# Third block of a four-block transformer: the norm's rows turned in the score-transposes' banks, projections in other slots, and another wait ahead of the MLP

## What is computed

```
ln_out = layernorm(x, ln1_s, ln1_b)
q, k, v = split(ln_out @ w_qkv + b_qkv)
x = x + merge(attention(q, k, v, ltor_mask)) @ w_ao + b_ao
ln_out = layernorm(x, ln2_s, ln2_b)
q = ln_out @ w_q + b_q
k, v = split(encoder @ w_kv + b_kv)
x = x + merge(attention(q, k, v, cross_mask)) @ w_co + b_co
ln_out = layernorm(x, ln3_s, ln3_b)
x = x + gelu(ln_out @ w1 + b1) @ w2 + b2
```

## Time and profile before

| | us |
|---|---|
| median of 3 runs | 1572.81 |
| profiled execution, its own time | 1579.1 |
| its span | 1577.3 |
| TensorE busy (matmuls) | 1481.9 |
| VectorE busy | 931.0 |
| ScalarE busy | 906.0 |
| POOL busy | 142.0 |

### The profile page before, as it was taken

How to read it: one execution, slowest core, us unless ns; L and a number is a source line. 1 busy time by engine, 2 the same in 40 slices (tenths; PEclk the granted TensorE clock), 3 DMA queues, 4 the chain that set the end, 5 groups by cost and what they waited for, 6 DMA issues and landing times.

```text
span 1577.3 us, 28655 instructions
## 1 busy us (share of the span) xinstructions
PE 1481.9 (94%) x9824; PEld 1140.7 (72%) x9824; DVE 931.0 (59%) x3314; ACT 906.0 (57%) x2807; POOL 142.0 (9%) x163
## 2 busy tenths in 40 slices
PE   7999999999999999999999999998888777999996
PEld 5766687788787877778788877786566556866664
DVE  4777723455554555445555445416999994168887
ACT  5888834434444444444444434435998895289996
POOL 2010010000000000000000000111122221022200
PEclk9999999999999999999999999999999999999999
DMA  7000103010010101001010000001000100000000
GB/s 288 1 2 2 59 5 120 1 48 15 1 62 1 62 1 47 15 1 61 1 47 16 1 1 1 1 1 54 1 2 8 41 9 7 1 1 8 22 2 15
DMA packets 10879, 40.66 MB, mean 26 GB/s; under 512 B 2416, under 2 KB 2672, under 8 KB 8688
## 3 DMA queue, kind: packets, MB, share of 16 engines
q1 hardware_dynamic: 10736, 38.82, 6.9%
HBM read 37.77 MB, written 1.05 MB: 25 GB/s over the span
## 4 chain that ended last, share of the span: by engine, by line
PE 68%; DVE 9%; ACT 9%; issue 3%; DVEq 0%; POOL 0%; POOLq 0%; ACTq 0%
PE bank L777 7%; PE bank L758 7%; PE bank L791 7%; PE bank L750 7%; PE bank L737 7%; PE bank L740 7%; ACT probs L948 6%; PE bank L706 5%; PE bank L717 5%; PE bank L766 4%; DVE probs L1201 3%; PE bank L562 3%; DVE probs L1183 3%; PE bank L549 2%; PE bank L584 2%
## 5 line engine op out<-in xcount | busy, mean ns | idle before, releaser
L948 ACT ACTIVATE probs<-probs,negmax 128x256 f32<-128x256 f32 (+1 forms) x640 | 347.3, 554 | 54.2 <-DVE negmax L1201 53.7
L1022 ACT ACTIVATE pT<-bank 128x512 f32<-128x512 f32 x128 | 76.4, 597 | 388.0 <-PE bank L766 388.0
L562 PEld LDWEIGHTS bank<-ident,probs 128*128 128x128 f32 x1536 | 170.4, 142 | 106.4 <-issue 52.1
L562 PE MATMUL bank<-ident,probs 128*128 128x128 f32 x1536 | 228.2, 282 | 19.4 <-ACT pT L956 14.9
L1334 DVE TENSOR_REDUCE stats<-bank 128x1 f32<-128x257 f32 x256 | 108.4, 425 | 212.4 <-PE bank L758 211.4
L1201 DVE CUSTOM_DVE_ANT_0 probs<-bank,mask_a 128x256 f32<-128x256 f32 (+1 forms) x384 | 174.2, 508 | 32.8 <-PE bank L549 28.1
L956 ACT ACTIVATE pT<-bank 128x512 f32<-128x512 f32 x288 | 169.8, 591 | 26.2 <-PE bank L562 25.3
L777 PE MATMUL bank<-pT,probs 128*128 128x256 f32 x512 | 132.7, 381 | 2.7 <-ACT pT L1022 2.7
L758 PE MATMUL bank<-kT,pT 128*128 128x257 f32 x512 | 132.7, 382 | 0.6 <-ACT pT L1005 0.6
L549 PE MATMUL bank<-kT,q_res 32*128 32x256 f32 (+1 forms) x1280 | 113.5, 460 | 19.7 <-DVE probs L1183 11.3
L948 ACT ACTIVATION_READ_ACCUMULATOR probs<-probs,negmax 128x1 f32 x640 | 129.3, 202 | 0.0
(11 more groups left out here) (110 smaller groups left out, 2485.4 us busy)
## 6 DMA issues: line engine op xcount, KB each, us to landing
w_m<-in_w SPq DMA_DIRECT2D x6, 1024.0 KB, 7.0
g_qkv<-in_g SPq DMA_DIRECT2D x4, 1536.0 KB, 7.6
q_res<-in_g SPq DMA_DIRECT2D x4, 1536.0 KB, 6.6
w_qkv<-in_w SPq DMA_DIRECT2D x3, 768.0 KB, 4.5
g_bv<-in_gbv SPq DMA_DIRECT2D x8, 256.0 KB, 7.2
g_o<-in_go SPq DMA_DIRECT2D x4, 512.0 KB, 3.4
q_res<-in_go SPq DMA_DIRECT2D x4, 512.0 KB, 3.5
rows<-in_rows SPq DMA_DIRECT2D x1, 1664.0 KB, 14.4
```

Of the source, the lines that this page charges most:

```text
L562: last = nc.tensor.transpose(out[:, n * P:(n + 1) * P], probs[:, u % PROBS, q * T + t * P:q * T + (t + 1) * P], ident[:, :])
L948: last = nc.scalar.activation(s, s, ACT.Exp, bias=negmax[:, u % PROBS, k:k + 1], scale=-1.0, accum_out=sums[:, tile % 2, q, j * c.res + r: ...
```

## The change

Within a part, q, k, y, v go to slots 1, 4, 8, 11. The norm's rows are turned at slot 2 (before: 1), for all parts but the last, in the bank into which that slot's unit is transposed afterwards (`turned_bank`, here always bank 5): TensorE waits for the copy of the unit two before, turns the rows, and the unit's transposes wait for ScalarE's take. ScalarE takes them before the exponential of slot 15 instead of behind that of slot 0. The last part's rows still use bank 7. The rows are written at the same VectorE slot (14), the bias added at the same POOL slot (15). In the MLP behind, slot 12 moves from f = 8 to f = 4, and TensorE waits at f = 0 for the masked products (`a_masked`) instead of the maxima.

```diff
     def y_slot(self, p):
-        return self.tile_slot(2 * p + 1) + (5 if self.kinds == "mult" else 4)
+        return self.tile_slot(2 * p + 1) + (2 if self.kinds == "mult" else 4)
     def norm_slot(self, p):
-        return self.y_slot(p) + 6
+        return self.y_slot(p) + (10 if self.kinds == "mult" else 6)
+    def rows_slot(self, p):
+        return self.after(self.y_slot(p) + 1) + (5 if self.kinds == "mult" else 2)
+    def between(self, p):
+        return self.kinds == "mult" and self.norm_slot(p) < self.count + self.turn_lag
+    def turned_bank(self, p):
+        return 4 + (self.norm_slot(p) - self.turn_lag) % 2 if self.between(p) else 7
...
-        at = [3, 6, 9] if self.kinds == "mult" else [2, 6, 14] if len(self.loads()) == 3 else [2, 6, 14, 22, 26]
+        at = [1, 4, 11] if self.kinds == "mult" else [2, 6, 14] if len(self.loads()) == 3 else [2, 6, 14, 22, 26]
...
-            out += [("n", p) for p in self.normed(slot)]
+            out += [("n", p) for p in self.normed(slot) if not self.between(p)]
...
                 def transposes(u):
                     pe.wait_ge(sem("a_exp"), st.at("a_exp", 0, u + 1))
-                    if u >= 2:
+                    rows = [p for p in c.normed(u + c.turn_lag) if c.between(p)]
+                    if rows:
+                        rows_turned(pe, *norm_of(rows[0]))
+                    elif u >= 2:
...
+                def normed_rows(p):
+                    u = c.norm_slot(p) - c.turn_lag
+                    if c.between(p):
+                        name, count = c.copied(u - 2)
+                        pe.wait_ge(sem(name), st.at(name, 0, count))
+                    else:
+                        free(c.use("n", p))
+                    turn_rows(*norm_of(p), bank[c.turned_bank(p)])
...
-                            for s in {1: [2, 3], 2: [4, 5, 6], 4: [7, 8, 9, 10, 11],
-                                      8: range(12, c.last_slot() - c.count + 1)}.get(f, []):
+                            for s in {1: [2, 3], 2: [4, 5, 6], 4: range(7, 13),
+                                      8: range(13, c.last_slot() - c.count + 1)}.get(f, []):
...
                             if b == 0 and f == 0 and n != 1:
-                                pe.wait_ge(sem("a_max"), end("a" + c.name, "a_max"))
+                                name = "a_masked" if c.kinds == "mult" else "a_max"
+                                pe.wait_ge(sem(name), end("a" + c.name, name))
...
                     if slot >= c.copy_lag and not c.by_vector(slot - c.copy_lag):
                         turned(slot - c.copy_lag)
+                    for p in c.normed(slot - c.copy_lag + 1 + c.turn_lag):
+                        if c.between(p):
+                            normed_rows(p)
                     if slot < c.count:
                         exps(slot)
...
-                        if c.after(c.y_slot(p) + 1) + 2 == slot:
+                        if c.rows_slot(p) == slot:
                             norm_rows(x.norm, x.b, dst)
...
-                    if slot == c.after(c.y_slot(p) + 1) + 3:
+                    if slot == c.rows_slot(p) + 1:
                         pool.wait_ge(sem("l_z"), S[x.norm].at("l_z", 0, x.b + 1))
```

More of the change, by code:

```diff
@@ L564, in transposes, with norm_of @@
                     last.then_inc(sem("a_t"), 1)
+                def norm_of(p):
+                    return (c.host, B - 1) if p < 0 else (c.parts[p].norm, c.parts[p].b)
+                def normed_rows(p):
[6 more added lines that the diff above has]
+                    turn_rows(*norm_of(p), bank[c.turned_bank(p)])
                 def times_v(vq):
@@ L625, in slot @@
                     for p in c.normed(s):
-                        free(c.use("n", p))
-                        name, b = (c.host, B - 1) if p < 0 else (c.parts[p].norm, c.parts[p].b)
-                        turn_rows(name, b, bank[7])
+                        normed_rows(p)
                     for vq in range(c.count // QUAD):
@@ L956, in turned, with normed_rows @@
                     nc.scalar.activation(pT[:, u % TURNED, :], bank[4 + u % 2][:, :], ACT.Copy).then_inc(sem("a_tout"), 1)
+                def normed_rows(p):
+                    name, b = (c.host, B - 1) if p < 0 else (c.parts[p].norm, c.parts[p].b)
+                    if NORMS[name][4] == "s":
+                        take_rows(name, b, bank[c.turned_bank(p)])
                 if c.name == "0":
@@ L968, in attention @@
                     for p in [p for x in range(ahead if slot else 0, ahead + 1) for p in c.normed(x)]:
-                        name, b = (c.host, B - 1) if p < 0 else (c.parts[p].norm, c.parts[p].b)
-                        if NORMS[name][4] == "s":
-                            take_rows(name, b, bank[7])
+                        if not c.between(p):
+                            normed_rows(p)
                     for what, p in c.projected(ahead) if ahead >= 0 else []:
```

## The result

The changed kernel takes **1550.86 us** (median of four runs, 1549.23 to 1552.42); the kernel before, timed beside it, 1575.31 us. The ratio is 0.985, with a 95% interval of 0.9835 to 0.9865: 24.4 us less. The forecast was 1552.0, in a range of 1549 to 1563, for 20.8 us less than 1572.81. The profiled execution took 1549.23 us, with a span of 1547.4, 29.9 shorter than the profiled one of before (1577.3). Not all of that is the change's. The first masked product of the block starts at 1081.37 us before and 1078.08 after, though nothing ahead of it was changed; in the windows view the granted clock of before was 0.96 in two of the 40 us windows up to there (160 to 200, 1000 to 1040), and after it was 1.00 in both.

The account below looks back on a forecast made before the run. VectorE was taken to set the attention's pace, idling in a loop of waits with TensorE and ScalarE. Savings of 10.9 + 2.9 + 7.0 = 20.8 us from 1572.8 gave 1552.0 us, range 1549 to 1563 (forecast's own 1549 to 1556).

Parts of the forecast that it names:

- Rows between units, cost nothing: Third block's attention: turning rows at slot 2 costs nothing, covered by VectorE's delay; 0 to 1.0 us a part otherwise.
- q, k, y, v: 1.82 us a part: Third block's attention: the new slots remove VectorE's idle time, 1.82 us in each of six parts, 10.9 us.
- all three waits: VectorE's idle time per part: 0.77 us for reciprocals, 0.58 for exponentials, 0.47 for v; all were to go.
- POOL: 0.41 us a part as before: Third block's attention: q's spreading on POOL still holds up VectorE's maxima by 0.41 us a part, bounds 0 to 2 x 1.07.
- the forecast's 28.05 us: Length of a part of the attention after the change; rows of the norm were to be 28.0 us apart.
- The MLP: 2.9 and 7.0 us: Behind the attention: 2.9 us from the earlier last product with v, 7.0 us from the earlier last y.
- the wait of 4.10 us: TensorE's wait after the last y, before the last norm's transposes; said to go whole.
- the clock, for which I had 2.9: TensorE's lower clock behind the wait after the last y; its removal was to save 2.9 us, bounds 0 to 2.9.
- The start of the block: First part: q fills TensorE's wait, k waits some 1.9 us for ScalarE, VectorE stays busy; nothing, -1 to +1 us.
- Rival A: Attention: POOL's spreading holds VectorE's maxima longer, taking back 4 to 10 us; 1556 to 1562 us, chance 0.15.
- Rival D: Attention: ScalarE waits for the rows before exponential 15 with its queue behind; slower, 1583 us at 6 us a place, chance 0.04.

Follow-up runs that it names:

- the later bias: Changed kernel with POOL's bias held back by one wait until the part's maxima are done; 1544.93 us, ratio 0.9813.
- The two single runs: Changed kernel with only one half of the attention change kept: rows only (1559.96 us) and slots only (1563.96 us).
- rows only: Changed kernel with q, k, v, y back in their old slots, rows still turned at slot 2; 1559.96 us, ratio 0.9897.
- slots only: Changed kernel with rows turned at slot 1 in bank 7, q and k in slots 3 and 6, y 8, v 11; 1563.96 us, ratio 0.9919.
- bias and masks later: Changed kernel with POOL's bias held until the part's maxima are done and additive masks until the eighth maximum; 1543.70 us, ratio 0.9799.
- the last y late: Changed kernel with the last part's y alone back in slots 139 and 140, rows turned at f = 8; 1558.37 us, ratio 0.9884.

## Why the prediction was right

The time, the sign and the range were right, and so was the place of each gain. That the time is off by only 1.1 us is in part luck. The saving was sized too small, 20.8 us where the stretch gives 23.5 and the medians 24.4, and it was taken from a median of 1572.81 that came out at 1575.31 with a fourth run. By its steps:

1. **Rows between units, cost nothing.** Right: waits of 0.37 and 0.34 us where 0.35 and 0 to 0.3 were said, both covered by VectorE. The prediction feared up to 1.0 us a part if the held maximum that covers the take went away. In the run with the later bias it did, and nothing of this came: the take waits for nothing, VectorE has no new wait and a part is shorter by the whole 1.07. What it costs when TensorE itself comes late to the rows, the run with the MLP's old wait shows.
2. **q, k, y, v: 1.82 us a part.** Right in kind: all three waits are gone from part 2 on; in part 1 the reciprocals' stays (0.93 us), so they give 10.2 us and not 10.9. But I gave the reason as the addition of y standing ahead of the inversion, with q freed of the take. The two single runs show that this isn't enough: with y forward and q and k in their old slots, q still waits 0.98 for the take and y 1.09 for k's copy; with the rows between units and the old slots, q doesn't wait and yet v's wait stays in every part.
3. **POOL: 0.41 us a part as before.** This term was wrong, and it is most of the 3.1 us by which the attention was undersized. The spreading now lies beside the masked products, and its 0.41 vanished; the additive masks hold up a maximum in three parts instead (0.87 us; such a part is 0.2 us longer), where I had named nothing. Over parts 1 to 6 that is 6 x 0.41 less 0.6, 1.9 us. Putting the spreading back at the maxima gives the forecast's 28.05 us. Part 0, for which I had taken nothing, gained about 1.8: before, three of its maxima were held up, by 0.41 beside the spreading and by 1.03 and 0.41 beside the bias and the mask that POOL does there once; with v moved out of the way none is, since other operations now lie beside POOL's. The single runs bear this out for bias and mask: with rows only, where v keeps its slot, they still hold a maximum by 1.04 and one by 0.41; with slots only, where v is the only projection moved in that part, none is held. The first 0.41, beside the spreading, is gone in both.
4. **The MLP: 2.9 and 7.0 us.** Measured 9.5 in all. The last product with v comes 2.4 us sooner behind the last maximum, not 2.9; the wait of 4.10 us is gone whole; what is left, about 3.0, I put down to the clock, for which I had 2.9. That part is a difference and was not isolated: putting y back cost the wait and only 1.5 of clock behind it, so the term varies from one execution to the next, and the full 2.9 was partly luck.
5. **The start of the block.** k waits for q's copy there as said, and VectorE never does: part 0 isn't longer.

Rival A has its mechanism right (POOL's reading holds maxima up) but not its place. The rule of the Trainium skill (SBUF — State Buffer, Who interferes with whom), that a VectorE instruction with two SBUF inputs waits for a whole GpSimd instruction that reads SBUF, is borne out by the bias: held 1.07 us, and released when the bias is moved beside masked products, which read only one SBUF tile. For the spreading no run shows a whole wait: each operation takes 1.6 to 2.1 us by POOL's rows, and no maximum lost more than 0.44. Rival D's danger, ScalarE waiting in front of the take, was seen nowhere in the attention, and for 3.04 us once, with the MLP's old wait. The 6.3 us between the profiled execution and the median of before, which I left unexplained, goes with the granted clock: of the 17 runs of before beside the later experiments, those with a mean of 0.996 took 1572.2 to 1572.3 us and those with 0.989 or 0.990 took 1578.7 to 1579.2; the profiled one had 0.990.

## What to carry to other kernels

When several in-order engines are each 84 to 92% busy, look for the operation that makes one queue wait for another in a ring, and move it where a wait is paid anyway; then see that its buffer and its neighbours' slots move with it, since one of the two alone may only trade waits. Look at which operation of one engine lies beside which of POOL: here 1.07 us a part was to be had for one semaphore wait. Price a long wait of TensorE with the slower matmuls behind it.

## What the runs showed that I had not expected

The granted clock does not follow from the wait alone. With the same wait of 1.86 us behind the last unit TensorE kept 1.00 in the changed kernel, with the spreading at the maxima and with bias and masks later, and fell to 0.50 with the last y late and with the bias later; behind 4.10 and 4.09 us it fell in both cases, for about 2.9 and 1.5 us of added time. Such a fall of 0.7 us is as large as what some of these edits are worth, so a difference between two profiled executions has to be looked up in their clocks first. And a held maximum isn't as long as POOL's operation: 1.07 us beside a bias of 1.39, 0.41 beside spreading operations of 1.6 to 2.1, about 0.45 beside a mask of 0.62.
